# Five stages instead of four, up-projections and turns further ahead, and pauses that end at the sixth result

## What is computed

```python
x = x + jnp.tanh(g_xattn[0]) * _L0_xattn_ref(_layernorm(x, axis=-1), ctx_512, ctx_512, ...)
x = x + jnp.tanh(g_ffn[0]) * _L0_ffn_ref(_layernorm(x, axis=-1), L0_ffn_Wr, L0_ffn_br, L0_ffn_W1, L0_ffn_W2)
# _L0_ffn_ref, of 8 experts:
route = jax.nn.sigmoid(x @ Wr + br)
max_prob = jnp.max(route, axis=1, keepdims=True)
max_ind = jnp.argmax(route, axis=1)
for e in range(n_experts):
    mask = (max_ind == e)[:, None].astype(x.dtype)
    y = jax.nn.gelu(x @ W1[e], approximate=False) @ W2[e]
    out = out + mask * y
out = out * max_prob
```

## Time and profile before

| | us |
|---|---|
| median of 3 runs (lowest, highest) | 149.15 (148.8, 150.14) |
| the profiled execution, its own time | 150.5 |
| its span, first to last instruction | 148.6 |
| TensorE (PE) busy | 132.3 (89%) |
| VectorE (DVE) busy | 96.4 (65%) |
| ScalarE (ACT) busy | 77.9 (52%) |
| GpSimd (POOL) busy | 121.3 (82%) |
| mean granted TensorE clock | 0.982 |

### The profile page before, as it was taken

How to read it: one execution, slowest core, us unless ns; L and a number is a source line. 1 busy time by engine, 2 the same in 40 slices (tenths; PEclk the granted TensorE clock), 3 DMA queues, 4 the chain that set the end, 5 groups by cost and what they waited for, 6 DMA issues and landing times.

```text
span 148.6 us, 4195 instructions
## 1 busy us (share of the span) xinstructions
PE 132.3 (89%) x1211; PEld 112.8 (76%) x1211; DVE 96.4 (65%) x532; ACT 77.9 (52%) x174; POOL 121.3 (82%) x198
## 2 busy tenths in 40 slices
PE   6989999989988976976899999999999999899690
PEld 2748777756755733854899899999999999899680
DVE  1698999997479999988659644455454345453230
ACT  0548597594584387328055274654555555454210
POOL 6538985887968988898998998998998998997354
PEclk9999999999999999999689999999999999999997
DMA  3999999911101151115413454551111100111000
GB/s 107 237 281 265 368 350 293 278 52 39 41 18 36 41 121 45 36 38 131 111 36 96 115 125 117 140 144 53 41 36 55 35 27 34 39 36 53 16 5 0
DMA packets 20080, 15.20 MB, mean 102 GB/s; under 512 B 6606, under 2 KB 16978, under 8 KB 20058
## 3 DMA queue, kind: packets, MB, share of 16 engines
q1 hardware_dynamic: 17328, 10.59, 27.2%
q0 software_dynamic: 2272, 4.27, 8.5%
q10 hardware_dynamic: 458, 0.08, 0.3%
HBM read 10.12 MB, written 5.26 MB: 103 GB/s over the span
## 4 chain that ended last, share of the span: by engine, by line
PE 53%; DVE 8%; issue 5%; POOL 1%; ACT 0%; DVEq 0%; POOLq 0%
PE banks_o L1309 24%; PE banks_v L1300 13%; PE bank_q L1300 5%; PE bank_p L1300 5%; PE bank_x L1292 3%; DVE rows L708 2%; PE bank_x L1172 1%; DVE stats L721 1%; POOL out_dram L448 1%; DVE tokn L926 1%; DVE rows L724 0%; DVE rows L775 0%; ACT hT L556 0%; DVE rank_max L742 0%; DVE tok L937 0%
## 5 line engine op out<-in xcount | busy, mean ns | idle before, releaser
L1309 PE MATMUL banks_o<-w_sb,hT 128*128 x312 | 42.6, 281 | 3.3 <-issue 1.8
L1309 PEld LDWEIGHTS banks_o<-w_sb,hT 128*128 128x128 f32 x312 | 38.5, 194 | 4.5 <-issue 4.4
L425 POOL DMA_INDIRECT scratch<-rows,row_at x32 | 31.8, 994 | 8.6 <-issue 4.5
L937 DVE SCALAR_TENSOR_TENSOR tok<-banks_o,tok 128x128 f32<-128x128 f32 x39 | 13.7, 350 | 35.3 <-PE banks_o L1309 22.5
L499 ACT COPY w_now<-w_sb 128x512 f32 x39 | 23.6, 611 | 10.3 <-issue 10.3
L442 POOL MEMSET unused<- 128x400 f32 x53 | 24.4, 461 | 0.0
L448 POOL DMA_INDIRECT out_dram<-tok x21 | 20.8, 991 | 3.5 <-issue 3.3
L448 POOL DMA_INDIRECT out_dram<-tok,token_at x18 | 17.7, 984 | 6.8 <-DVE tok L937 4.0
L1300 PE MATMUL banks_v<-toknT,w_now 128*128 128x128 f32 x160 | 22.0, 282 | 0.0
L556 ACT ACTIVATE hT<-banks_v 128x512 f32<-128x512 f32 x20 | 11.9, 596 | 17.5 <-PE banks_v L1300 10.7
L1300 PEld LDWEIGHTS banks_v<-toknT,w_now 128*128 128x128 f32 x160 | 20.3, 199 | 0.0
(11 more groups left out here) (176 smaller groups left out, 245.7 us busy)
## 6 DMA issues: line engine op xcount, KB each, us to landing
tok<-scratch SPq DMA_DIRECT2D x39, 66.0 KB, 2.2
x_all<-in_x_dram SPq DMA_DIRECT2D x8, 256.0 KB, 4.4
w_sb<-in_L_ffn_W_dram SPq DMA_DIRECT2D x1, 2048.0 KB, 10.5
ctx<-in_ctx_dram SPq DMA_DIRECT2D x8, 128.0 KB, 4.3
scratch<-pad_rows SPq DMA_DIRECT2D x1, 528.0 KB
scratch<-rows,row_at POOLq DMA_INDIRECT x32
out_dram<-tok POOLq DMA_INDIRECT x21
out_dram<-tok,token_at POOLq DMA_INDIRECT x18
```

What stands on the lines that cost most here:

```text
L425: nc.gpsimd.indirect_dma_start(out=scratch, out_offset=bass.IndirectOffsetOnAxis(ap=row_at[:, g * GT + t:g * GT + t + 1], axis=0), in_=row ...
L937: nc.vector.scalar_tensor_tensor(out=tok[j][:, 0:D], in0=y_ps[j % 2], scalar=tok[j][:, SCALE:TOKEN], in1=tok[j][:, 0:D], op0=ALU.mult, op1 ...
L1309: last = nc.tensor.matmul(y_ps[j % 2], hT[j % DEEP][:, c * P:(c + 1) * P], w2_sb[:, bass.ds(w_at[j] + c * D, D)], start=(c == 0), stop=(c ...
```

## The change

- `STAGES` has five entries: tiles 5 to 8 after four groups, 9 to 12 after five; the batches' stages follow. The tables of the first two stages are now both made inside the attention loop, in VectorE's turns k = 6 and k = 7; the third and fourth in its loop over j.
- The four fillers after D(0) and after D(1) are gone. T(5) comes straight after D(1), with U(4) behind it, the counts and prefixes stand after D(1) and D(3), and routing and tables are spread anew over VectorE's j = 0 to 8.
- `lead` is 3 up to D(6), 2 from D(7) to D(16), and 3 from D(17) on, so that two up-projections follow D(16).
- From U(24) on (`FAR` = 24) tiles are turned two ahead of the up-projection, in turn into bank_x and bank_s, with three `tokn`.
- `PAUSED` is 6.

```diff
-    STAGES = [(NG - 5, 5), (NG - 3, 13), (NG - 1, 21), (NG, FFN_TILES)]
+    STAGES = [(NG - 5, 5), (NG - 4, 9), (NG - 3, 13), (NG - 1, 21), (NG, FFN_TILES)]
...
-    BATCHES = [(0, 0, 5), (1, 5, 4), (1, 9, 4), (2, 13, 4), (2, 17, 4), (3, 21, 6), (3, 27, 6), (3, 33, 6)]
+    BATCHES = [(0, 0, 5), (1, 5, 4), (2, 9, 4), (3, 13, 4), (3, 17, 4), (4, 21, 6), (4, 27, 6), (4, 33, 6)]
...
+    FAR = STAGE_TILES[LAST_STAGE][0] + 3
...
-    PAUSED = FFN_TILES - 8
+    PAUSED = 6
...
-        tokn = [sb(f"tokn_{i}", [P, D]) for i in range(2)]
+        tokn = [sb(f"tokn_{i}", [P, D]) for i in range(3)]
...
+                                             (banks_o[:, 0, :], 2 * VW + 2 * E),
...
-        tT_ps = bank_x[:, 0:P]
+        tT_ps = [bank_x[:, 0:P], bank_s[:, 0:P]]
...
+        def turn_bank(j):
+            return 1 if j > FAR and (j - FAR) % 2 else 0
...
         def lead(j):
-            return 3 if j < 7 else 2
+            return 2 if 7 <= j < 17 else 3
...
+        def turned(n):
+            return 1 if n < FAR else 2
...
-                    after(dve, toknT_done, j - 2)
-                    nc.vector.tensor_scalar(tokn[j % 2][:], tok[j][:, 0:D], tok[j][:, MEAN:RSTD], tok[j][:, RSTD:SCALE],
+                    after(dve, toknT_done, j - 3)
+                    nc.vector.tensor_scalar(tokn[j % 3][:], tok[j][:, 0:D], tok[j][:, MEAN:RSTD], tok[j][:, RSTD:SCALE],
                                             ALU.subtract, ALU.mult).then_inc(tokn_ready, 1)
 
...
-                    nc.vector.tensor_copy(toknT[j % DEEP][:], tT_ps).then_inc(toknT_copied, 1)
+                    nc.vector.tensor_copy(toknT[j % DEEP][:], tT_ps[turn_bank(j)]).then_inc(toknT_copied, 1)
...
-                if k == NG - 2:
-                    copy_counts(0)
+                if k >= NG - 2:
+                    copy_counts(k - (NG - 2))
...
+                if k == NG - 1:
+                    take_tiles(0)
...
-                if k == NG - 2:
-                    count_tiles(0)
+                if k >= NG - 2:
+                    count_tiles(k - (NG - 2))
...
-                if k == NG - 2:
-                    count_left(0)
+                if k >= NG - 2:
+                    count_left(k - (NG - 2))
...
-                if k == NG - 2:
-                    sum_tiles(0)
+                if k >= NG - 2:
+                    sum_tiles(k - (NG - 2))
...
-                if k == NG - 2:
-                    pass_experts(0)
-                    move_rows(0)
-                    place_tiles(0)
-                if k == NG - 1:
-                    take_tiles(0)
+                if k >= NG - 2:
+                    pass_experts(k - (NG - 2))
+                    move_rows(k - (NG - 2))
+                    place_tiles(k - (NG - 2))
...
-            copy_counts(1)
+            copy_counts(2)
...
-            count_tiles(1)
             place_of_group(NG - 3)
             variance2(NG - 1)
             place_rows(NG - 3)
-            count_left(1)
+            take_tiles(1)
             scale_logits(NG - 2)
             copy_transposed(3)
             bias_logits(NG - 2)
-            sum_tiles(1)
             normalise_tile(4)
-            pass_experts(1)
             for j in range(FFN_TILES):
                 residual2(j)
+                for n in range(j + lead(j), j + 1 + lead(j + 1)):
+                    for m in range(n + turned(n - 1), n + 1 + turned(n)):
+                        copy_transposed(m)
+                        if j > 0:
+                            normalise_tile(m + 1)
+                if j == 0:
+                    for step in range(7):
+                        choose(NG - 2, step)
+                    normalise_tile(5)
                 if j == 1:
 
                     count_tiles(2)
@@ -1117,51 +1133,46 @@
                     count_left(2)
                     bias_logits(NG - 1)
                     sum_tiles(2)
-                    choose(NG - 1, 0)
-                    pass_experts(2)
-                    choose(NG - 1, 1)
-                    normalise_tile(5)
-                    choose(NG - 1, 2)
-                    move_rows(2)
-                for n in range(j + lead(j), j + 1 + lead(j + 1)):
-                    copy_transposed(n + 1)
-                    if j > 0:
-                        normalise_tile(n + 2)
-                if j == 0:
-                    move_rows(1)
-                    choose(NG - 2, 0)
-                    choose(NG - 2, 1)
-                    place_tiles(1)
-                    choose(NG - 2, 2)
-                    choose(NG - 2, 3)
-                    choose(NG - 2, 4)
-                    choose(NG - 2, 5)
-                    choose(NG - 2, 6)
-                    take_tiles(1)
                     place_of_group(NG - 2)
                     place_rows(NG - 2)
-                    copy_counts(2)
-                if j == 1:
+                    copy_counts(3)
+                if j == 2:
+                    pass_experts(2)
+                    choose(NG - 1, 0)
+                    choose(NG - 1, 1)
+                    move_rows(2)
+                    choose(NG - 1, 2)
                     choose(NG - 1, 3)
+                    place_tiles(2)
                     choose(NG - 1, 4)
                     choose(NG - 1, 5)
                     choose(NG - 1, 6)
-                    place_tiles(2)
+                if j == 3:
                     take_tiles(2)
-                if j == 2:
                     place_of_group(NG - 1)
                     place_rows(NG - 1)
-                    copy_counts(3)
-                if j == 3:
+                    copy_counts(4)
+                if j == 4:
+
                     count_tiles(3)
                     count_left(3)
                     sum_tiles(3)
                     pass_experts(3)
-                if j == 4:
+                if j == 5:
                     move_rows(3)
+                    place_tiles(3)
+                    take_tiles(3)
+                if j == 6:
+
+                    count_tiles(4)
+                    count_left(4)
+                    sum_tiles(4)
+                    pass_experts(4)
+                if j == 7:
+                    move_rows(4)
                     find_last_rows()
-                if j == 5:
-                    place_tiles(3)
+                if j == 8:
+                    place_tiles(4)
                     shift_last_tiles()
...
-                    after(pe, toknT_copied, j - 1)
-                    nc.tensor.transpose(tT_ps, tokn[j % 2][:], ident[:]).then_inc(toknT_done, 1)
+                    if turn_bank(j):
+                        pe.wait_ge(skip_ready, 1)
+                    after(pe, toknT_copied, j - 1 if j <= FAR + 1 else j - 2)
+                    nc.tensor.transpose(tT_ps[turn_bank(j)], tokn[j % 3][:], ident[:]).then_inc(toknT_done, 1)
...
-            pe.wait_ge(counts_copied, 2)
+            pe.wait_ge(counts_copied, 3)
...
+                for n in range(j + lead(j), j + 1 + lead(j + 1)):
+                    for m in range(n + turned(n - 1), n + 1 + turned(n)):
+                        transpose_tile(m)
+                    up(n)
                 if j == 1:
-
-                    up(4)
-                    keep_busy(4, bank_x)
-                    transpose_tile(5)
-                    continue
-                for n in range(j + lead(j), j + 1 + lead(j + 1)):
-                    transpose_tile(n + 1)
-                    up(n)
-                if j == 0:
-                    pe.wait_ge(toknT_copied, 5)
-                    keep_busy(4, bank_x)
                     pe.wait_ge(placed, NG - 2)
                     count_groups(LAST_STAGE - 1)
                     prefix(NG - 2)
-                if j == 2:
+                if j == 3:
                     pe.wait_ge(placed, NG - 1)
                     pe.wait_ge(counts_copied, LAST_STAGE)
                     count_groups(LAST_STAGE)
```

## The result

The changed kernel takes 160.57 us (median of four, 159.39 to 161.57) against 149.12 us for the kernel before beside it: ratio 1.0728, 95% interval 1.0665 to 1.0791. The forecast was 146.5 us, faster. It is 7% slower.

What follows compares the result with a forecast made beforehand. TensorE was taken as the bound from 82.2 to 137.3 us, waiting from 62.2 to 82.2. Earlier down-projections (-3.1) and a later tail (+0.4) gave -2.7 from 149.15: 146.45, say 146.5 us, range 145.6 to 147.5.

Steps and rivals of the forecast that it cites:

- The step that failed: GpSimd's result scatters: cutting pauses from result 6 on is worth nothing itself, but keeps the 3.1 us from being lost.
- D36's wait of 1.25 us: Down-projection 36 waiting for a Gelu in the profiled execution: left out as an event not counted on.
- D0: First down-projection: moves from 62.21 to 63.8 us; later than 65 would show the prediction wrong.
- VectorE's added work: Last turn of the attention loop, with the added stage table: 1.55 us more, between 1.1 and 2.0.
- rival 1: Hand-over before the first tile turn: the clock falls to half, costing about 1.4 us, 147.9 us in all; chance 0.15.
- D0 to D7: Down-projections 0 to 7 in the rewritten order: 15.3 us instead of 19.97, the last 3.1 us earlier at 79.1.
- From D7 on: Down-projections 7 to 36: TensorE bounds the steady part, no turn or up-projection waits for data; 57.0 to 57.6 us.
- Three ahead and early turns: Up-projections three ahead from tile 17, turns two ahead from tile 24: worth nothing in the steady part.
- rival 2: Register loads in TensorE's queue: three ahead hides them, -1.4 us, 145.1 us in all; chance 0.10.
- The tail: Last scatter begins 3.0 us after down-projection 38 begins, instead of 2.6: 0.4 us later, bounds 0 and 0.9.
- The slower rival: From 94 to 131 us GpSimd's issues shut VectorE out: 0.15 us more per tile, +4.2, 150.7 us; chance 0.08.
- The port rule: VectorE in two-port modes and GpSimd lock each other out of shared ports; normalising could wait out 0.98 us.

Runs made afterwards that it cites:

- before_without_pauses_3: Kernel before with only the pauses from result 6 on taken out, run on chip 15: 159.2 us, ratio 1.0445.
- after_stages_only: Kernel before with five stages, the new order of work and three tokn; lead, turns and pauses as before: 147.92 us, ratio 1.0026.
- before_without_pauses: Kernel before with only the pauses from result 6 on taken out, first run: 147.45 us, ratio 0.9974.
- stages_and_fillers: Kernel before with the new stages and order, pauses kept, plus ten filler matmuls at the end of the routing: 151.9 us, ratio 1.0006.
- after_with_pauses: Changed kernel with its pauses put back up to result 30, first run: 149.2 us, ratio 1.0096.
- before_lead_and_turns_only: Kernel before with lead 3 from tile 17 and turns two ahead from tile 24, stages and pauses as before: 149.23 us, ratio 1.005.
- after_with_pauses_3: Changed kernel with its pauses put back up to result 30, run on chip 15: 153.51 us, ratio 1.0109.
- after_pauses_16_again: Changed kernel with pauses behind results 0 to 15, run again on a chip with irregular loads: 154.26 us, ratio 1.0206.
- after_3: Changed kernel word for word, run again on chip 15 beside the kernel before: 162.45 us, ratio 1.069.

## Why the prediction was wrong

**The step that failed** is "It is off the path, so the removal is worth nothing by itself". GpSimd was off the path, and still its rate decided. I looked for the cost of that rate on VectorE only. It lies in TensorE's signals. On the chips that show it, a signal of TensorE's comes up to 9 us late while GpSimd issues a scatter each 1.29 or 1.43 us. What it delays waits, in most profiles until the backlog is gone, and the standing brings 6.83 us of half clock behind it. That the pauses decide this is shown by two kernels on chip 15; why the signals are late is not shown.

**The sign stood in my own rows.** I set D36's wait of 1.25 us aside as an event "that I don't count on". It comes in the only place where the kernel before issues results without pauses. GpSimd, ScalarE and VectorE of the kernel before:

```profile
136.72 0.98 POOL L448 DMA_INDIRECT out_dram<-tok,token_at  x1 [0.30 <-issue]
138.09 0.98 POOL L448 DMA_INDIRECT out_dram<-tok,token_at  x1 [0.39 <-issue]
...
139.87 0.60 ACT L556 ACTIVATE hT<-bank_q 128x512 f32<-128x512 f32 x1 [3.68 <-PE banks_v L1300]
...
139.97 0.35 DVE L937 SCALAR_TENSOR_TENSOR tok<-banks_o,tok 128x128 f32<-128x128 f32 x1 [2.15 <-remote]
```

Unpaused scatters, a Gelu 3.68 us idle, a "remote" wait of VectorE that ends 0.9 us after the last scatter: the hole in small. U36's signal is updated at 139.85, 2.4 us after its product. It was the one visible price of running without pauses, and I took it for noise.

**D0** came at 65.03, not 63.8, above the bound that I named as wrong. Two terms. VectorE's added work was sized 1.55: on chip 15, both at full clock, D0 is 63.61 with the new stages (and ten fillers) and 61.54 in before_without_pauses_3, so 2.07, just over my upper end of 2.0. And rival 1 came true, with 6.83 us of half clock in the hand-over where I had 3.4; the fillers show it to be worth 0.8 us.

**D0 to D7** was right step by step, waits included (T5 and D2 stand 0.50 and 0.46 us): forecast +1.9, 5.3, 7.2, 9.9, 11.8, 13.9 and 15.3; measured +1.89, 5.30, 7.30, 10.02, 12.01, 14.02 and 15.25. But what that gains depends on what it is compared with. On chip 11 D7 stands at 80.50 in after_stages_only and 81.23 in before_without_pauses: 0.7 us, not 3.1. On chip 15, where the kernel before keeps its clock, it stands at 79.99 with stages and fillers and 79.88 in before_without_pauses_3: nothing.

**From D7 on** I took TensorE as the bound at once. It is not yet. The table of the last stage now stands between tiles 7 and 11 on VectorE. This is T11 and D9 in after_stages_only:

```profile
83.73 0.33 PE L1305 MATMUL bank_x<-ident,tokn 128*128 128x128 f32 x1 [0.27 <-DVE tokn L936]
...
84.79 1.06 PE L1322 MATMUL banks_o<-w_sb,hT 128*128 x8
```

D7 to D17 is 19.82 us there, and 19.13 in before_without_pauses on the same chip: 0.7 us, all that the stages had brought on it. That is why they alone give 1.0026. D7 itself was thus early only beside a kernel before whose clock fell to half for 3.41 us, as in the earlier trace rows.

**Three ahead and early turns** were put at nothing. From D16 to D38 they take 43.90 us (after_with_pauses) against 42.25 (after_stages_only), 1.65 more on one chip. The extra U behind D16 costs 1.12 and comes back at the end, where D35 to D38 takes 3.57 us for 4.61. D18 to D19 takes 0.33 more, for a reason that I did not follow. The largest part that does not come back, 1.2 us, lies at T26, the first turn that must follow another within one step. In the changed kernel:

```profile
121.11 0.27 PE L1305 MATMUL bank_s<-ident,tokn 128*128 128x128 f32 x1
122.17 0.33 PE L1305 MATMUL bank_x<-ident,tokn 128*128 128x128 f32 x1 [0.79 <-DVE tokn L936]
```

VectorE starts to normalise tile 26 at 121.78, behind the residual of tile 21 (121.32) and the copy of T25 (121.59), both of which wait for TensorE. The step D21 to D22 takes 3.02 to 3.15 us in every other kernel with these turns (3.67 in before_lead_and_turns_only), and 1.90 without them. In the whole times the part is smaller: 1.3 us (149.2 against 147.92), and 1.005 alone. I had written that in the steady part no T waits for data. I had not followed the one step in which two turns meet. The stops for registers didn't shrink, so rival 2 is false: D18 comes 2.37 us after D17 with three ahead as with two.

**The tail** was right: the last scatter begins at 155.00, 3.03 us after D38 at 151.97; forecast 3.0. That the full pauses would hold up the end was right too, though smaller: in after_stages_only the last eight scatters follow each other at 1.29 us, and the last begins 3.53 us after D38 (144.20 after 140.67), for 2.60 in before_without_pauses.

**The slower rival** had the side and the place (from 94 us, while GpSimd catches up) but not the mechanism. Line 936 takes 340 ns at the median and 866 at most in the changed kernel, against 341 and 828, nowhere near the 1.2 us from which it would decide. The port rule that stood beside it (the Trainium skill, "SBUF — State Buffer", section "Who interferes with whom") explains nothing of the hole: VectorE's instructions are not longer there, they are missing. So I had a rival for the right place with a chance of 0.08 and no price above 4.2 us.

Against the forecast of -2.7 us, then, the changed kernel with its pauses shows +1.4 to +1.7 us (ratios 1.0096, 1.0115 and 1.0109): D0 to D17 about nothing in place of -3.1, lead and turns +1.65 in place of 0 up to D38. The missing pauses add 8.9 us to it on chip 15, seen on the same chip; on chips 2 and 11 the changed kernel itself was never run.

No version is faster than the kernel before by more than can be measured. stages_and_fillers stands at 1.0006, and before_without_pauses at 0.995 to 0.997 on two chips and 1.0445 on a third.

## What to carry to other kernels

Before you take out a wait or a pause because its engine is off the path, ask what its rate touches besides the path: look in the trace for places where that engine already runs without it, and read every late instruction there (above all "remote") as a price, not as noise. When two kernels disagree, run them side by side on one chip: a set of four kernels went into a partner that did not exist, because the one kernel that spoke against the plain theory had run on another chip. And where work is pulled ahead, follow the one step at which the distance changes, since two dependent turns meet in it.

## What the runs showed that I had not expected

- Chips differ in kind, not only in speed. On chips 2 and 11, 19 scatters 1.29 us apart leave TensorE busy 23.1 of 23.3 us, and from 60 us on no recorded update of TensorE's is more than 0.04 us late in any of the eight profiles. On chips 13, 15 and that of the first set, all nine profiles of kernels with a long row of results 1.43 us apart or less have the hole, with a longest delay of 4.9 to 9.0 us, and SyncE's loads come irregularly. With 1.59 us the delays are smaller but not nil: a step D14 to D15 of 3.09 us in after_with_pauses_3, and delays of up to 2.5 us from 75 us on in before_without_pauses_3, where the pauses still stood. This may be most of why the kernel before takes 149.1 to 152.6 us on such chips and 147.2 to 147.6 on the others. What in the chip makes the difference is open, and so is whether the signals wait in a queue behind GpSimd's writes or somewhere else: no row shows the way that they take. Nor is it shown that the hole would be there without the profiler, which is an open rival: every run on record carries a span and a clock, and on the chips with holes the trace itself holds only 57 to 73% of the semaphore updates of TensorE, VectorE and ScalarE from 60 us on, on chips 2 and 11 98 to 100%.
- The long delay mostly ends about when GpSimd stops. In the changed kernel VectorE resumes at 107.35 with 15 results done and the 15th scatter over at 105.74; in before_without_pauses_3 at 103.61 with 13 and 102.16; in after_pauses_16_again at 121.74 with 23 and 120.43. In seven of the nine profiles this is 1.3 to 1.6 us behind the end of that scatter, and in after_3 it is during it; with pauses of 200 columns the longest delay ended before the backlog was gone. Shorter delays of 2 to 5 us stand before the long one in most of them.
- The granted clock fell to half in or behind every hole, for 3.41 to 10.24 us. In the hand-over it stood at half for 6.83 or 10.24 us in the kernels with the new stages (3.41 in two of them), and ten fillers of 128x512 kept it at 1.00 in the profile of stages_and_fillers.
